# First attention of a macaron block on one core: values and decayed keys formed by VectorE from the PSUM bank, and the next feed-forward's first chunk quantised inside the attention's last four tiles

## The reference

```
x = x + 0.5 * L0_ffn(layernorm(x))        # weights and activations rounded to an FP4 grid in blocks of 16
x = x + L0_attn(layernorm(x))             # the stage that is changed
x = x + 0.5 * L0_ffn(layernorm(x))        # its first chunk is now prepared earlier
x = x + 0.5 * L1_ffn(layernorm(x))
x = x + L1_attn(layernorm(x))
x = x + 0.5 * L1_ffn(layernorm(x))
```

```
q, k, v = split(x @ Wqkv.T + b);  k = k * SCALE;  g = sigmoid(gamma_raw)
state = g * state + outer(v_t, k_t);   y_t = state @ q_t;   out = y @ out_w.T + out_b
```

## Time and profile before

| | |
|---|---|
| median of 3 runs | 2746.56 us (2735.77 to 2752.08) |
| the profiled execution | 2748.86 us, of which the span is 2746.9 us |
| PE, DVE, ACT, POOL busy | 93%, 66%, 50%, 41% of the span |
| first attention | about 567 us to 1009.2 us of the span |
| second feed-forward starts its matmuls | 1031.4 us |

### The profile page before, as it was taken

How to read it: one execution, slowest core, us unless ns; L and a number is a source line. 1 busy time by engine, 2 the same in 40 slices (tenths; PEclk the granted TensorE clock), 3 DMA queues, 4 the chain that set the end, 5 groups by cost and what they waited for, 6 DMA issues and landing times.

```text
span 2746.9 us, 75964 instructions
## 1 busy us (share of the span) xinstructions
PE 2565.8 (93%) x31464; PEld 2156.2 (78%) x31464; DVE 1802.2 (66%) x4190; ACT 1374.9 (50%) x2281; POOL 1123.0 (41%) x1382
## 2 busy tenths in 40 slices
PE   4999999989989969999999899999999999979999
PEld 3878788777778757877888688887888888858888
DVE  7887788545655558889887566644565666645664
ACT  4444444344444424444444588864444544418886
POOL 5555555423333325555554423211444344462221
PEclk9999999999999989999999999999999999979999
DMA  5000000000101010000000000000000000000001
GB/s 176 1 6 1 1 1 1 1 16 22 23 21 22 22 50 1 1 1 1 1 1 1 17 1 1 1 7 19 17 19 16 17 17 18 18 5 24 31 32 39
DMA packets 67557, 45.85 MB, mean 17 GB/s; under 512 B 13184, under 2 KB 66192, under 8 KB 67216
## 3 DMA queue, kind: packets, MB, share of 16 engines
q1 hardware_dynamic: 67216, 41.00, 5.5%
HBM read 15.78 MB, written 8.40 MB: 9 GB/s over the span
## 4 chain that ended last, share of the span: by engine, by line
PE 34%; issue 12%; POOL 9%; DVE 5%; ACT 3%; SPq 0%; DMA 0%; POOLq 0%; DVEq 0%; ACTq 0%
PE ps L593 5%; PE ps L1376 4%; PE ps L1377 4%; PE ps L1391 3%; PE ps L1393 3%; PE ps L46 3%; PE ps L48 3%; PE ps L47 3%; PE ps L248 2%; POOL a1pry L1945 2%; POOL a1pry L1947 2%; POOL a1l L1933 2%; DVE XTL L258 2%; POOL a1P L1941 1%; POOL a1pry L1941 1%
## 5 line engine op out<-in xcount | busy, mean ns | idle before, releaser
L593 PE MATMUL ps<-WDT,fHT 128*128 128x256 f32 (+1 forms) x1536 | 386.1, 394 | 8.7 <-ACT fHT L644 8.7
L593 PEld LDWEIGHTS ps<-WDT,fHT 128*128 128x128 f32 (+1 forms) x1536 | 283.5, 192 | 82.4 <-issue 42.8
L1443 DVE TENSOR_TENSOR gHl<-gHf,gHh 128x512 fp32r<-128x512 f32 x256 | 190.7, 745 | 210.1 <-ACT gHh L1420 209.8
L726 POOL TENSOR_TENSOR fV<-fH,frc 128x704 f32<-128x704 f32 x128 | 178.1, 1391 | 343.4 <-DVE frc L715 343.4
L46 PE MATMUL ps<-WGH,XTH 128*128 128x512 f32 (+1 forms) x768 | 313.8, 409 | 2.8 <-DVE XTL L258 1.4
L48 PE MATMUL ps<-WGL,XTH 128*128 128x512 f32 (+1 forms) x768 | 290.3, 378 | 0.0
L47 PE MATMUL ps<-WGH,XTL 128*128 128x512 f32 (+1 forms) x768 | 289.8, 377 | 0.0
L1391 PE MATMUL ps<-W2T,gHh 128*128 128x256 f32 x1024 | 257.2, 284 | 0.0
L1393 PE MATMUL ps<-W2T,gHl 128*128 128x256 f32 x1024 | 254.4, 280 | 0.0
L1376 PE MATMUL ps<-XTH,W1T 128*128 128x512 f32 x512 | 207.7, 406 | 20.5 <-DVE XTL L258 18.6
L638 ACT ACTIVATE ps<-fV 128x704 fp32r<-128x704 f32 x128 | 97.5, 762 | 256.2 <-DVE fV L292 248.3
(11 more groups left out here) (225 smaller groups left out, 6386.4 us busy)
## 6 DMA issues: line engine op xcount, KB each, us to landing
X<-in_x SPq DMA_DIRECT2D x16, 512.0 KB, 8.9
a0vp<-a0vt SPq DMA_DIRECT2D x256, 32.0 KB, 1.9
a1vp<-a1vk SPq DMA_DIRECT2D x256, 32.0 KB, 2.2
out<-X SPq DMA_DIRECT2D x16, 512.0 KB, 2.9
tws<-in_w SPq DMA_DIRECT2D x2, 1024.0 KB, 7.6
WN<-in_wgu SPq DMA_DIRECT2D x3, 384.0 KB, 5.4
a0km<-in_wqkv SPq DMA_DIRECT2D x2, 384.0 KB, 3.3
a1pry<-in_aw SPq DMA_DIRECT2D x1, 768.0 KB, 4.6
```

What stands on the lines that cost most here:

```text
L593: h = pe.matmul(down, HT[n % 2][0:m, c, :], WDT[0:m, c, :], start=(c == 0), stop=(c == 5))
L726: pool.tensor_tensor(s3(V[(n - 1) % 2][:, :]), s3(H[(n - 1) % 2][:, :]), cast16(rc[(n - 1) % 2][:, :], 44), ALU.mult).then_inc(s_hv, 1)
L1443: dve.tensor_tensor(Hl[m % 8][:, :], Hf[m % 4][:, :], Hh[m % 8][:, :].bitcast(F32), ALU.subtract).then_inc(s_hl, 1)
```

## The change

Three edits.

1. `VK` is gone, and with it ACT's copy and POOL's two operations. DVE does both from the PSUM bank in a new function `held(n)`, ahead of `decay(n)`. The bank is released by `s_kp` (DVE) where it was by `s_vr` (ACT). A space of the same size keeps all other buffers where they were.
2. `stats`, `spread` and `norm` of the feed-forward's chunks 0 and 1 run inside the attention (tiles 58 and 59, 62 and 63), as those of the attention's own chunks do.
3. Chunk 0 is quantised inside the last four tiles: `x_scale` and `x_value` at tile 60, `x_mag` at 61, `x_grid` at 61 and 62, `x_scaled` at 62, transposes, `XTH` and `XTL` at 63. The maxima lie in the query buffer `QT[0]` and the magnitudes in `QP[0]` (SBUF), where they were in a PSUM bank. Of the `before_*` functions only the zeroing of a PSUM area and the first steps of chunk 1 remain.

```diff
+            def held(n):
+                bank = bank0("v", n)
+                dve.wait_ge(s_kx, n + 1)
+                if n > 2:
+                    dve.wait_ge(d_vp[(n - 3) % 2], 64 * ((n - 3) // 2) + 64)
+                    dve.wait_ge(s_up, grown(2 * (n - 3) + 1))
+                dve.tensor_tensor(Vt[n % 3][:, :], bank[:, 0:256], bvt[:, :], ALU.add).then_inc(s_vt, 1)
+                if n > 1:
+                    dve.wait_ge(s_up, grown(2 * (n - 2) + 1))
+                dve.tensor_tensor(a0KP[n % 2][:, :]..., bank[:, 256:512]..., KD[:, :]..., ALU.mult).then_inc(s_kp, 1)
...
             for n in range(NT + 2):                      # DVE
                 if n < NT:
+                    held(n)
                     decay(n)
                     state(2 * n)
...
-                if n < NT and j == 2 and i + 2 < NS:
+                if n < NT and j == 2:
                     for k in range(8):
-                        stats(dve, 1, i + 2, k)
+                        stats(dve, *chunk(16 + i + 2), k)
...
+                if n == NT - 4:
+                    dve.wait_ge(s_sc, 4 * (NT - 5) + 4)
+                    x_scale(dve, 2, 0)
+                if n in (NT - 3, NT - 2):
+                    x_grid(dve, 2, 0, n - NT + 3)
+                if n == NT - 1:
+                    low(NS)
...
-                    act.activation(VK[n % 2][:, :], bank0("v", n)[:, :], ACT.Copy).then_inc(s_vr, 1)
...
-                pool.tensor_tensor(Vt[n % 3][:, :], VK[n % 2][:, 0:256], bvt[:, :], ALU.add).then_inc(s_vt, 1)
-                pool.tensor_tensor(a0KP[n % 2][:, :]..., VK[n % 2][:, 256:512]..., KD[:, :]..., ALU.mult).then_inc(s_kp, 1)
+                if j == 2:
+                    spread(pool, *chunk(16 + i + 2))
+                if n == NT - 4:
+                    x_value(pool, 2, 0)
+                if n == NT - 2:
+                    x_scaled(pool, 2, 0)
...
+                if n == NT - 1:                          # PE, after the output projection of tile 61
+                    turn_x(NS)                           # waits for x_scaled of chunk 0
...
+xam = lambda S, i: QT[0][:, 0, 0:64] if S and i == 0 else PS[3][:, 0:64]
+xmag = lambda S, i, h: QP[0][:, h, :] if S and i == 0 else PS[3]
```

More of the change, by code:

```diff
@@ L98, in macaron @@
         a0A = [sb(a0, f"a0A{i}", [P, 1024]) for i in range(2)]
-        VK = [sb(a0, f"a0vk{i}", [P, 512]) for i in range(2)]
+        sb(a0, "a0gap", [P, 1024])
         QT = [sb(a0, "a0qt0", [P, 2, 512]), QTb]
@@ L323, in x_mag @@
                 act.wait_ge(s_qxq, 2 * g + 1)
-            act.activation(xmag.bitcast(R32), XV[:, 512 * h:512 * h + 512], ACT.Abs, scale=MAGIC).then_inc(s_qxa, 1)
+            act.activation(xmag(S, i, h).bitcast(R32), XV[:, 512 * h:512 * h + 512], ACT.Abs, scale=MAGIC).then_inc(s_qxa, 1)
         def x_grid(dve, S, i, h):
@@ L355, in x_low, with before_dve, before_act, before_pool @@
             low_dve(dve, 16 * S + i, k, PS[3])
-        def before_dve(dve, S):
+        def before_dve(dve):
             dve.memset(PSA[64:128, 3712:3840], 0.0).then_inc(s_hz, 1)
[L360 to L386, removed]
+            x_scale(dve, 2, 1)
+        def before_act(act):
+            x_mag(act, 2, 1, 0)
+        def before_pool(pool):
+            x_value(pool, 2, 1)
+        def before_pe(pe):
             pe.wait_ge(s_hz, 2)
-            for k in range(2):
-                x_turn_pe(pe, S, 0, k)
         s_wam, s_wsn, s_wrc, s_wv = sem("wam"), sem("wsn"), sem("wrc"), sem("wv")
@@ L778, in slots0 @@
                                 2: [("p", i, 2), ("p", i, 3)], 3: []}[n % 4]
+                if n == NT - 1:
+                    yield from [("t", i, 0), ("t", i, 1)]
         ring0 = numbered(slots0())
@@ L918, in turn_x @@
                     bank = take("t", i, k)
-                    if k == 0:
+                    if k == 0 and i < NS:
                         pe.wait_ge(s_xn, 16 + i + 1)
-                    turn_pe(pe, 16 + i, k, bank, xf)
+                    if k == 0 and i == NS:
+                        pe.wait_ge(s_qxx, 17)
+                    turn_pe(pe, 16 + i, k, bank, xf if i < NS else XV)
             def proj(i, os):
@@ L1084, in attn0_act @@
                     act.activation(a0YT[m % 2][:, :], PS[6][:, 0:256], ACT.Copy).then_inc(s_ye, 1)
-                if n < NT and j == 3 and i + 2 < NS:
-                    norm(act, 1, i + 2)
+                if n < NT and j == 3:
+                    norm(act, *chunk(16 + i + 2))
                 if n < NT and i + 1 < NS:
@@ L1093, in attn0_act @@
                         proj(i + 1, (2, 3))
+                if n == NT - 3:
+                    act.wait_ge(s_it, entered(2 * (NT - 5) + 1))
+                    x_mag(act, 2, 0, 0)
+                    x_mag(act, 2, 0, 1)
+                if n == NT - 1:
+                    turn_x(NS)
         def attn0_dve(dve):
@@ L1969, in _ @@
             attn0_end(act)
-            before_act(act, 2)
+            before_act(act)
             ffn0_act(act, 2)
@@ L1999, in _ @@
             attn0_end(dve)
-            before_dve(dve, 2)
+            before_dve(dve)
             ffn0_dve(dve, 2)
@@ L2014, in _ @@
             attn0_end(pe)
-            before_pe(pe, 2)
+            before_pe(pe)
             ffn0_pe(pe, 2)
```

37 lines of the change are left out of this document (12 added, 25 removed).

## The result

The changed kernel took 2707.59 us (median of 4 runs, 2706.46 to 2709.44) against 2749.32 of the kernel before beside it, 41.7 us less: a ratio of 0.9857, 95% interval 0.9821 to 0.9893. Run again later (e9) it took 2704.50 against 2744.29, a ratio of 0.9862 (0.9840 to 0.9884). Predicted were 2703 us and a range of 2692 to 2721.

What follows compares the result with a forecast made beforehand. PE was taken to bound the attention, busy 403.8 of 440.2 us. The terms, -25.9 - 1.4 - 0.5 + 3.9 + 0.9 - 21.6 = -44.6, took 2748.9 to 2704.3, set at 2703 us; range 2692 to 2721.

Steps and rivals of the forecast that it cites:

- Terms 1, 2 and 3: Attention: grow's waits for POOL, -25.9 us; three DMA waits of values, -1.4; first tile's further grow wait, -0.5.
- the ring's bank: Fourth tile of a group: grow's second bank, emptied by ACT, would be free 0.56 us before grow starts.
- Terms 4 and 5: Attention's end: chunk 0's early work delays the last sum, +3.9 us; x_grid blocked beside POOL's spread, +0.9.
- Term 6: Gap between the attention's last sum and the feed-forward's first matmul: from 22.2 to about 0.6 us, -21.6.
- B: Attention's groups of four tiles: held stands behind DVE's queue, half the feeding gain lost, 13 us, 2716; chance 0.14.
- C: Attention's end: DVE's waits over tiles 61 to 63 10 us, not 4.8, low clock +2: 2711; chance 0.10.
- D: Attention's end and after: x_grid not blocked and a clock that stays up, 2698 us; chance 0.08.
- E: Every attention tile: held late, PE waits for DVE at grow, 92 us on top, 2796; chance 0.03.
- term 1: Attention: grow's 25 waits for POOL's decayed keys, 27.7 us, shrink to 0.07 us each, -25.9 us.

Runs made afterwards that it cites:

- e9: The changed kernel as it is, run again beside the two reordered ones on one chip; 2704.50 us against 2744.29 of the kernel before, ratio 0.9862.
- e1: The kernel before with only the first edit: VectorE takes values and decayed keys from the bank, nothing prepared early; 2718.48 us, ratio 0.9901.
- e5: The changed kernel with held(n) moved behind decay(n) in VectorE's list; 2738.94 us in one run, beside 2740.42 of the kernel before.
- e4: The changed kernel with one more VectorE product in every held, ahead of the real one, into an unused buffer; 2700.96 us, ratio 0.9837.
- e3: The changed kernel with statistics, spread and norm of chunk 1 taken behind the rest of tile 63; 2700.47 us, ratio 0.9834.
- e8: The changed kernel with the early work on chunk 0 and part of chunk 1 spread over more tiles, from 55; 2696.73 us, ratio 0.9839.
- e11: The kernel of e8 run again for a direct comparison; 2693.91 us, ratio 0.9818.
- e2: The changed kernel with the bank again emptied by ScalarE and GpSimd, chunk 0 still prepared in the last four tiles; 2734.80 us, ratio 0.9964.
- e7: The changed kernel with 64 small matmuls added to PE's list in tile 0; 2716.32 us in one run.
- e12: The changed kernel with 32 small matmuls added to PE's list in tile 0; 2706.38 us in one run.

## Why the prediction was right, and where a size was off

The time came inside the range and near the forecast, and the mechanism of each large term is the one described. Some sizes inside it were off.

**Terms 1, 2 and 3, the feeding of PE.** The mechanism is as described: e1 shows it alone, e5 shows that the place ahead of `decay` is its condition, e4 that the margins are there. `held` took 0.75 us (0.78 predicted), the ring's bank was free 0.56 us ahead (0.56 predicted). The size was off: from the first scores to those of tile 60 it is 567.4 to 986.5 before and 567.5 to 962.3 after, 24.3 us less where the terms came to 27.8. The mis-sized term is the first. I let each wait shrink to 0.07 us and put nothing in for PE's pauses for instructions: they rose from 6.3 to 9.8 us. That this is just the 3.5 that is missing is partly luck. Over the eight traces with `held` ahead of `decay` and with nothing added to the lists of PE and the DMAs (the changed kernel, e1, e3, e4, e8 to e11), the gain was 21.4 to 25.9 us and the pauses came to 8.9 to 13.3.

Before, the waits had hidden part of the pauses. The strongest sign is e5, where `grow` waits in 63 tiles: its list of waits has no pause at all. In e2, with the waits for POOL back, the pauses were 6.0 us. As the weight loads see it, the kernel before had nine pauses. The changed one has six of them at the same places, not the ones at 569.6, 583.4 and 592.0, and new ones. Those at 750.2 and 960.0 stand in tiles in which `grow` had waited 1.3 us for POOL; those at 627.1, 841.5 and 918.7 stand in a tile without such a wait, but the tile in front of each had one of 0.3 to 0.6 us. That the pauses are fetches is shown by e7 and e12; why a given fetch comes late stays open.

**Terms 4 and 5, the end of the attention.** +4.8 predicted, 27.7 - 22.7 = +5.0 measured, but by other parts. `grow(61)` and `grow(62)` did not wait, and `grow(63)` waited 1.40 us and not 2.4: `held(63)` ended 18.4 us behind tile 60's scores, where I had added up 19.9. In place of that, PE's clock fell behind the wait, which I had only as a bound, and only for the feed-forward's start. PE was busy 25.0 us of these 27.7; in e3, without the wait and at a clock of 1.00, 22.5 of 23.5. The difference, about 2.5 us, is my estimate of what the clock cost. And `x_grid` was not held up: its halves took 0.66 and 0.69 us beside `spread`. GpSimd lost instead: its power (the `rs` row) took 1.45 us where it took 1.04 in the kernel before. Later in the same tile VectorE lost, 1.46 us for a pair of `state` beside `x_scaled`, where 0.41 is normal. The Trainium skill ("SBUF — State Buffer", SBUF: two separate sides) says of the port pair that whichever operation starts first has it for the whole instruction and the other blocks fully. Both rows agree: `x_grid` had started before the power, `x_scaled` before the second `state`, which ended 0.22 us behind it. I had taken the rule as a loss for VectorE alone. That the two terms together came out right, at 5.0, was chance.

**Term 6, the gap.** 22.2 to 0.7, -21.5 where -21.6 was predicted. Chunk 1 kept its distance: its transposes wait 2.27 us for `x_scaled`, as before, C is 518.3 in both, and the better clock at the feed-forward's start (0.94 granted over 28 us, against 0.87) brought nothing, as reckoned.

**The rivals.** B, half of the feeding gain lost to waits of `grow`, is excluded by the waits: one wait for VectorE, in tile 63. C, an end that costs double, did not come: the end cost 5.0 us and not 10, and the low clock stood in the last tile and not at the feed-forward's start. D did not come; e8 and e11 show that something like it was to be had by spreading the work. E was a matter of one position in a list (e5).

**The signs.** Of those that I had named for being right, two came short: the attention lasted 421.0 us from 569 and not 417, and `grow(63)` waited 1.4 us and not 2 to 4. The first is the miss of term 1. None of the signs for being wrong came: a half of `x_grid` took 1.35 us, the gap was 0.7 us, and the last three stages differed by 1.3 us.

**The sum.** -24.3 + 5.0 - 21.5 = -40.8 against -44.6, and behind the feed-forward's first matmul the traces differ by 1.3 us more, inside the scatter of those stages. The median was 2707.6 where 2703 was predicted.

## What to carry to other kernels

Where an engine in the middle of a chain is late, look for another that is idle in just that window, and put the work at the head of its list: one place further made the attention 47 us longer here (e5). Two edits that share an engine are to be priced together, since one can be what makes room for the other. And where PE runs many small matmuls, as here, its waits can hide pauses for instructions; here waits reckoned at 27.8 us gave back 21 to 26.

## What the runs showed of the hardware

- PE's instructions came in packets of 16 KB, 256 instructions each (e7), and in stretches of small matmuls PE paused 0.2 to 1.6 us at fixed places of the stream: 6.3 us over the attention of the kernel before, 9.8 and 13.3 in the two traces of the changed one, 15.4 in e7, and nothing in e5, where PE waits in nearly every tile.
- PE's wait of 1.40 us at tile 63 was followed by a granted clock of 0.50 (1.2 GHz) from 980.9 to 987.7; without the wait (e3, e8) the clock stayed at 1.00. Not every such wait does this: of the 26 waits for POOL in the kernel before, up to 1.8 us long, two were followed by the low clock, from 823.6 and from 902.1, and so was the pause of 1.31 us that ended at 676.4.
- A GpSimd and a VectorE operation on SBUF delayed each other in both directions; each time the one that had started later took longer: GpSimd's power 1.45 us where it took 1.04 before, VectorE's pair of `state` 1.46 where 0.41 is normal.
